# A decoder layer on one core: ScalarE as a second emptier of PSUM banks, the first tile's lines kept on chip, one bias folded into another, and a newly drawn order

## The chip, the cores and the metric

The kernel runs on one core of a Trainium2 chip. The metric is the device time of one execution, in microseconds (us), as the median of several runs. A core has TensorE (PE, matrix products, writes PSUM), VectorE (DVE), ScalarE (ACT), GpSimd (POOL) and SyncE (SP, which here only issues DMAs). Each engine works through its own queue in order; engines wait for each other by semaphores.

## The reference

One decoder layer over x (2048 tokens, 256 features) with a context of 1601 tokens, in float32. The middle step of the first part is what the change touches most.

```python
x = x + self_attn(layernorm(x)); x = x + cross_attn(layernorm(x), ctx); x = x + moe(layernorm(x))

# self attention, 16 heads: queries and keys are six-number "lines"
q1 = bg @ W1_q.T; q2 = bg @ W2_q.T            # bg = [x, previous row of x]; 4 numbers per head
k1 = x @ W1_k.T;  k2 = x @ W2_k.T
q = lines(q1, q2); k = lines(k1, k2)          # p1[i]*p2[j] - p1[j]*p2[i] over 6 pairs, divided by its norm
attn = softmax(causal(einsum(q, J6 k)) * 6**-0.5)
v = x @ Wv.T + bv
out = (attn @ v) @ Wo.T + bo
# cross attention: 16 heads of 16 features, softmax(q k^T) v over 1601 keys, output projection + bias
# moe: 16 experts of 64 tokens, chosen from 6 rounds of Sinkhorn normalisation, gelu, scatter-add
```

## The kernel before

The 2048 tokens are four tiles of 512 tokens, each of four blocks of 128. The work of all engines comes from one list, PLAN, which build_plan() draws up before the kernel is built: it holds ten streams of steps (x, lines, ctx, keys, ones, max, query, weights, scores, pv) with assumed costs, and again and again takes the step whose weighted cost is lowest. Every engine then walks the same PLAN and issues its part of each step. The weights W set the order; nothing is reordered at run time.

The steps that matter here:

- **prep of a tile**: load four blocks of x (`x_load`, SP), mean and variance (`stats`, DVE, and a power on POOL), `norm` (DVE, L1177), `x_turn` (PE transposes into a PSUM bank, L1651; DVE copies it to `xn_t`, L1187), `project` (PE, L1660 and L1663: the line components and the values of a block; DVE adds the value bias bv into `v_self`, L1198, and copies the components to `raw`, L1201). `carry` and `carry_out` hand the last column of one tile to the next.
- **lines of a tile**: three parts on DVE. Part 0 is 24 products of 128x64 (L1218, L1220) for a tile. Part 1 subtracts, sums the squares and takes 1/sqrt by an integer start and three Newton steps of four instructions (L1119 to L1125). Part 2 scales and splits each number into three bf16 parts (L1234 to L1238) in `line_parts`, which lies in even_region. `line_turn` (PE, L1670, a block each) transposes the parts, DVE copies them (L1246), SP stores them to `line_d` in DRAM (L841), and `line_load` brings them back in another arrangement, 24 small DMAs a tile (L741), to `q_line` and `k_line` in self_region: 36 rows, six slots of six components. The products of the slots add up to a product of nearly float32 accuracy. For tile 0 SP and ACT issue 12 of the loads each.
- **ctx_k, ctx_v**: keys and values of the context (PE, L1636, L1645). DVE splits the keys into three parts (`split`: L1139, L1140, L1142, L1143), SP stores them (L802). `x_query` is the same for the queries of the cross attention.
- **scores, pv**: a quad is a group of four heads on one block of keys. PE makes the scores of two heads (L1588 self, L1584 cross) in one of two PSUM buffers, ACT takes the exponential to `probs` (L1050), POOL masks the diagonal block in the self attention (L979), PE multiplies with the values into the bank `po` (L1608). ACT empties `po` after each group of four heads (L1062).
- **join**: `o_turn`, `a_turn`, `out_proj` turn the attention's output, divide it by its sum and project it; DVE empties all three. bo is added to xb by POOL (`bias`, L955) before that.
- **max**: the score maxima of the cross attention, 1024 banks, each four small matmuls (L1702) and a reduction on DVE (L1294).
- After the last pv come the router and the experts, in fixed order.

Ten kinds of step share three PSUM banks g0 to g2 in rotation (G_USE counts them; `g_full` says that PE has filled one, `g_free` that DVE has emptied one). All are emptied by DVE, in PLAN's order. So a bank that DVE empties late holds PE up three uses later. The first self scores wait for all 24 loads of tile 0.

## Time and profile before

| | us |
|---|---|
| median of 3 runs | 1194.92 |
| the runs | 1191.08 to 1196.68 |
| the profiled execution's own time | 1202.16 |
| its span | 1200.4 |
| PE busy | 1110.4 (93%) |
| DVE busy | 874.8 (73%) |
| ACT busy | 708.1 (59%) |
| POOL busy | 153.7 (13%) |
| first self scores on PE | 90.62 |
| mean granted TensorE clock (share of full) | 0.965 |

The profile describes one execution, which lies 7.24 us above the median of the runs. Its busy times count an engine as busy from an instruction's start to its end; PE's overlap in a pipeline. "PEclk" is the clock that TensorE was granted, 1.00 being 2.4 GHz. A name such as cross_region or even_region covers several tensors that share the memory: ctx_sb, parts_ctx and line_t lie in cross_region, raw, lines and line_parts in even_region. The idle time behind an instruction in square brackets is that of its engine just before it, with what ended it.

### The profile page before, as it was taken

How to read it: one execution, taken by the hardware profiler on the slowest of the kernel's cores; microseconds unless marked ns; L12 is line 12 of the kernel's file. 1: busy time of each engine (PE TensorE's matmuls, PEld its weight loads, DVE VectorE, ACT ScalarE, POOL GpSimd, SP SyncE). 2: the span in 40 equal slices, each digit the busy share in tenths (PEclk: the TensorE clock that was granted, in tenths of full speed). 3: DMA queues.
4: the chain of work that ended last, by engine and by line, in shares of the span. 5: the costliest groups of instructions: out<-in, count | busy, mean ns of one | idle time of the engine just before them, and what ended most of it. 6: DMA issues, size and time to landing. Idle time of an engine off the chain costs nothing.

```text
span 1200.4 us, 30294 instructions
## 1 busy us (share of the span) xinstructions
PE 1110.4 (93%) x12556; PEld 519.3 (43%) x12556; DVE 874.8 (73%) x2062; ACT 708.1 (59%) x792; POOL 153.7 (13%) x260
## 2 busy tenths in 40 slices
PE   4677998999999999999999999999999999788797
PEld 2342442332333333444555455555454442566354
DVE  5888458378878888898888888788888980477431
ACT  0005648787767877667866787677775789110011
POOL 3005243212101111000001000010001000101322
PEclk8886899999999999999999999999999999998899
DMA  4141268511111000104122201111111000195794
GB/s 169 31 129 46 80 110 120 134 45 46 33 35 57 16 15 1 51 21 138 30 94 70 91 13 30 51 47 30 30 29 54 16 16 2 42 365 119 214 353 106
DMA packets 85080, 92.32 MB, mean 77 GB/s; under 512 B 20448, under 2 KB 77472, under 8 KB 84944
## 3 DMA queue, kind: packets, MB, share of 16 engines
q1 hardware_dynamic: 78568, 81.35, 24.2%
q10 hardware_dynamic: 4584, 6.88, 1.8%
q0 software_dynamic: 1792, 2.16, 1.0%
q8 instruction: 99, 1.62, 0.6%
q14 instruction: 37, 0.30, 0.1%
HBM read 74.73 MB, written 15.63 MB: 75 GB/s over the span
## 4 chain that ended last, share of the span: by engine, by line
PE 80%; DVE 11%; issue 3%; ACT 3%; POOL 1%; another core or an unknown queue 1%; DMA 0%; SPq 0%; DVEq 0%; ACTq 0%
PE po L1608 24%; PE g L1702 16%; PE scores L1584 14%; PE scores L1588 6%; PE g L1687 3%; ACT probs L1050 3%; PE g L1817 2%; PE g L1793 2%; PE g L1660 2%; PE g L1651 2%; PE g L1677 1%; PE g L1693 1%; PE scores L1617 1%; POOL probs L979 1%; PE g L1670 1%
## 5 line engine op out<-in xcount | busy, mean ns | idle before, releaser
L1050 ACT ACTIVATE probs<-scores 128x1024 f32<-128x1024 f32 (+2 forms) x736 | 676.7, 967 | 297.4 <-PE scores L1588 160.8
L1294 DVE TENSOR_REDUCE mx<-g 128x1 f32<-128x400 f32 (+1 forms) x1024 | 527.2, 568 | 73.3 <-PE g L1702 63.2
L1702 PE MATMUL g<-cross_region,even_region 96*32 96x400 bf16 (+1 forms) x4096 | 306.2, 336 | 0.2
L1584 PE MATMUL scores<-even_region,cross_region 99*32 99x512 bf16 (+1 forms) x3264 | 251.9, 379 | 4.4 <-ACT probs L1050 4.4
L1608 PE MATMUL po<-probs,cross_region 128*32 128x512 f32 (+1 forms) x1664 | 223.2, 593 | 0.8 <-ACT probs L1050 0.8
L1702 PEld LDWEIGHTS g<-cross_region,even_region 96*32 96x32 bf16 x4096 | 118.7, 95 | 179.5 <-DVE mx L1294 74.1
L1608 PE MATMUL po<-probs,self_region 128*32 128x512 f32 (+3 forms) x1280 | 155.1, 559 | 8.7 <-POOL probs L979 8.0
L1584 PEld LDWEIGHTS scores<-even_region,cross_region 99*32 99x32 bf16 (+1 forms) x3264 | 96.0, 96 | 104.5 <-issue 47.3
L1588 PE MATMUL scores<-self_region 36*128 36x512 bf16 (+3 forms) x640 | 107.0, 361 | 7.7 <-ACT probs L1050 7.1
L947 POOL TENSOR_TENSOR rstd<-mv,half 128x1 f32<-128x1 f32 x48 | 27.2, 566 | 586.7 <-DVE mv L1135 586.4
L979 POOL TENSOR_SCALAR_AFFINE_SELECT probs<-probs 128x256 f32<-128x256 f32 x128 | 61.9, 491 | 263.4 <-ACT probs L1050 262.7
L1588 PEld LDWEIGHTS scores<-self_region 36*128 36x128 bf16 x640 | 27.7, 94 | 130.1 <-ACT probs L1050 89.5
L1608 PEld LDWEIGHTS po<-probs,cross_region 128*32 128x32 f32 (+1 forms) x1664 | 55.8, 110 | 25.6 <-ACT probs L1050 4.0
L1085 ACT ACTIVATE even_region<-scores 128x1024 f32<-128x1024 f32 x4 | 4.1, 1024 | 94.6 <-remote 71.0
L1617 PE MATMUL scores<-xbo_sb,ident 128*128 128x256 f32 x190 | 51.1, 422 | 0.0
L1608 PEld LDWEIGHTS po<-probs,self_region 128*32 128x32 f32 x1280 | 30.8, 111 | 39.7 <-POOL probs L979 17.1
L1651 PE MATMUL g<-ident,xn 128*128 128x128 f32 x96 | 21.7, 310 | 27.5 <-DVE xn L1177 25.4
L1268 DVE RECIPROCAL rsum<-g 128x16 f32<-128x16 f32 x32 | 8.1, 255 | 48.2 <-PE g L1677 48.0
L1617 PEld LDWEIGHTS scores<-xbo_sb,ident 128*128 128x128 f32 x190 | 39.2, 213 | 6.2 <-issue 0.2
L1279 DVE TENSOR_TENSOR xb<-g,xb 128x256 f32<-128x256 f32 x32 | 13.6, 425 | 32.1 <-PE g L1687 31.3
L1660 PE MATMUL g<-wself_sb,xn_t 128*128 128x512 f32 x64 | 33.5, 649 | 2.4 <-DVE rest L1140 2.4
L1187 DVE COPY xn_t<-g 128x256 f32<-128x256 f32 x48 | 20.2, 421 | 17.2 <-PE g L1651 17.0
(270 smaller groups left out, 878.4 us busy)
## 6 DMA issues: line engine op xcount, KB each, us to landing
cross_region<-in_w SPq DMA_DIRECT2D x16, 1024.0 KB, 12.1
even_region<-xq_d SPq DMA_DIRECT2D x192, 64.0 KB, 2.3
self_region<-in_w ACTq DMA_DIRECT2D x6, 1024.0 KB, 8.7
self_region<-in_w SPq DMA_DIRECT2D x6, 1024.0 KB, 13.3
cross_region<-xk_d SPq DMA_DIRECT2D x24, 200.1 KB, 10.2
xb<-in_x SPq DMA_DIRECT2D x32, 128.0 KB, 3.0
xb<-x_d SPq DMA_DIRECT2D x32, 128.0 KB, 2.4
probs<-in_w SPq DMA_DIRECT2D x4, 1024.0 KB, 13.0
```

Of the source, the lines that this page charges most:

```text
L947: pool.tensor_tensor(rstd[:, u % 4:u % 4 + 1], mv[:, u % 4, 1:2], half[:, 0:1], ALU.pow).then_inc(rstd_ready, 1)
L979: pool.affine_select(out=d, in_=d, compare_op=ALU.is_ge, fill=0.0, base=0, pattern=[[0, 2], [1, P]], channel_multiplier=-1).then_inc(mask_ ...
L1050: act.activation(probs[0:rows, s % 4, :, off:], ps[s % 2][0:rows, :, off:], ACT.Exp, scale=LSCALE if QUADS[n][0] == "self" else 1.0).then_ ...
L1294: dve.reduce_max(mx[:, k % 2, b, h, c:c + 1], g[:, 0:n_keys], AX_X).then_inc(g_free, 1)
L1584: mm = pe.matmul(ps[s % 2][c:c + n_keys, a, :], k_cross[0:NS * DH + 3, h, i * P + c:i * P + c + n_keys], rhs, start=True, stop=True)
L1588: mm = pe.matmul(ps[s % 2][0:rows, a, off:], lhs, rhs, start=True, stop=True)
L1608: mm = pe.matmul(po[32 * a:32 * a + 32, off:], v[0:rows, i, h * VW:h * VW + 32], probs[0:rows, s % 4, a % 2, off:], start=(i == 0), stop=e ...
L1617: pe.matmul(ps[0][:, 0, 0:D], ident[:, :], xbo_sb[:, :], start=True, stop=True)
L1651: mm = pe.transpose(g[:, k * P:(k + 1) * P], xn[:, norm_no[u] % 2, k * P:(k + 1) * P], ident[:, :])
L1660: pe.matmul(g[:, :], xn_t[:, k, c + 1:c + 1 + P], wself_sb[:, k, 0:512], start=(k == 0), stop=False)
L1687: mm = pe.matmul(g[:, 0:D], attn_t[:, k, :], (wo_sb if step[1] == "self" else wxo_sb)[:, k, :], start=(k == 0), stop=(k == DK - 1))
L1702: mm = pe.matmul(g[q:q + 32, 0:n_keys], q_max[k % 2][0:NS * DH, h, b * P + q:b * P + q + 32], k_cross[0:NS * DH, 4 * (k % 4) + h, start:st ...
```

## The change

1. **ACT as a second emptier.** For nine kinds of step (ctx_k, x_query, ctx_v, x_turn, project, line_turn, a_turn, gate, slot_turn) the planner chooses DVE or ACT (`BY[step]`). A second semaphore `g_free_act` counts ACT's, and `wait_freed` waits for the right one. A split that ACT shares is cast by ACT, subtracted by DVE, cast again by ACT, subtracted by DVE.
2. **Tile 0's lines stay on chip.** In place of line_turn, store and load, ACT copies the query parts and DVE the key parts, 12 copies of 128x192 each, into the slot arrangement in `probs` (`copy_to_slots`); PE transposes that directly, 8 steps of 8 transposes (`slot_turn`), each emptied by one copy of 100x1024 to `q_line` or `k_line`. The unused columns are zeroed once at the start.
3. **bv into bo.** Since the weights of a softmax row add up to one, bv @ Wo is added once to bo (`bias_row`: two matmuls and an addition). The values are then only copied.
4. **Lines.** Part 0 takes 16 products in place of 24 (three pairs that share component 0 go in one instruction). A Newton step is three instructions (two scalar_tensor_tensor) in place of four. `raw` may be overwritten once part 0 has read it (`raw_read`).
5. **Small moves.** bv and log_temp are loaded from ACT's queue as columns. `carry_out` comes earlier; the last one is dropped.
6. **Order.** The weights W are others, and the costs and conditions in the planner follow the points above.

```diff
@@ planner
-W = dict(start=0.252, hungry=2.38, fed=0.0138, act_near=0.2601, max=2.2344, max_ahead=0.05, max_from=72.59,
+W = dict(hungry=0.714, fed=0.0083, act_near=0.2211, max=3.7538, max_ahead=0.0147, max_from=72.59, max_end=8.352,
...
-    x_steps = prep(0) + prep(1) + prep(2) + join("self", 0) + prep(3) + query(0)
+    x_steps = prep(0) + prep(1) + [("bias_row",)] + prep(2) + join("self", 0) + prep(3) + query(0)
...
+        if j == 0:
+            line_steps += [("slots", j)] + [("slot_turn", b, side) for b in range(BPT) for side in range(2)]
+            continue
...
+                if step[0] in EITHER:
+                    got = place(step, free, "ACT")
+                    choices.append((name, step, got, "ACT", W["act_late"] if ("scores", 0) in at else W["act_early"]))
@@ waiting for a bank
+        def wait_freed(eng, *steps):
+            for sm in (g_free, g_free_act):
+                counts = [FREED[st][1] for st in steps if FREED[st][0] is sm]
+                if counts:
+                    eng.wait_ge(sm, max(counts))
@@ slots
+        def copy_to_slots(copy, side):
+
+            for s, part in enumerate((Q_SLOTS, K_SLOTS)[side]):
+                src = line_parts.rearrange("p (b s) q (a e c) -> p b s q a e c", s=2, e=2, c=NC)
+                dst = slotted.rearrange("p s (b a) c -> p s b a c", b=BPT)
+                for e in range(2):
+                    c = 64 * e + s * NC
+                    last = copy(dst[:, side, :, :, c:c + NC], src[:, :, side, part, :, e, :])
+            return last
@@ ScalarE
-            act.wait_ge(s_w["rest"], 112)
+            def empty(step):
...
+                elif kind == "project":
+                    b = step[1]
+                    act.wait_ge(v_ones, 4)
+                    if b >= BPT:
+                        act.wait_ge(raw_read, b // BPT)
+                    act.copy(v_self[:, b, 0:H * VW].rearrange("p (h v) -> p h v", h=H)[:, :, 0:DH],
+                             g[:, 256:512].rearrange("p (h d) -> p h d", h=H))
+                    act.copy(raw[:, b % BPT, :], g[:, 0:256]).then_inc(g_free_act, 1)
...
+                elif step == ("slots", 0):
+                    act.wait_ge(lines_split, 1)
+                    last = copy_to_slots(act.copy, 0)
+                    last.then_inc(slots_q, 1)
...
-                elif step == ("line_load", 0, 1):
-
-                    for r in range(4):
-                        act.wait_ge(line_stored[r], 16)
-                    load_line_side(act, 0, 1)
@@ VectorE
                 for _ in range(3):
                     link(dve.tensor_tensor(t, y, y, ALU.mult))
-                    link(dve.tensor_tensor(t, t, v, ALU.mult))
-                    link(dve.tensor_scalar(t, t, -0.5, 1.5, ALU.mult, ALU.add))
-                    link(dve.tensor_tensor(y, y, t, ALU.mult))
+                    link(dve.scalar_tensor_tensor(out=t, in0=t, scalar=-0.5, in1=v, op0=ALU.mult, op1=ALU.mult))
+                    link(dve.scalar_tensor_tensor(out=y, in0=t, scalar=1.5, in1=y, op0=ALU.add, op1=ALU.mult))
...
+            dve.memset(slotted.rearrange("p s n c -> p (s n) c")[:, :, NS * NC:64], 0.0).then_inc(v_ones, 1)
+            dve.wait_ge(s_w["bv"], 16 * DK)
+            dve.tensor_copy(attn_t[:, :, :], bv_col.unsqueeze(2).broadcast_to((P, DK, P))).then_inc(bias_col, 1)
...
+                            dve.tensor_tensor(lv[:, :, side, :, near], one[:, :, :, 0:1].broadcast_to((P, BPT, H, 3)),
+                                              two[:, :, :, 1:4], ALU.mult)
@@ TensorE
                 if kind == "self" and g == 0 and i == 0 and e == 0:
-                    pe.wait_ge(lines_loaded[j], 16 * 24)
+                    if j:
+                        pe.wait_ge(lines_loaded[j], 16 * 24)
+                    else:
+                        wait_freed(pe, *[("slot_turn", b, side) for b in range(BPT) for side in range(2)])
...
+                    for a in range(H // 2):
+                        mm = pe.transpose(gb[0:100, a * P:(a + 1) * P], slotted[:, side, b * H // 2 + a, :], identb[:, :])
```

TensorE's queue up to the first self scores, before. x_turn is `g<-ident,xn`, project `wself_sb,xn_t`, ctx_k and ctx_v `g<-cross_region`; this is the part behind tile 1's projections:

```order
L1651 MATMUL g<-ident,xn 128x128 x4
L1636 MATMUL g<-cross_region 128x512 x2
L1645 MATMUL g<-cross_region 128x256 x8
L1670 MATMUL g<-identb,even_region 96x128 x24
L1636 MATMUL g<-cross_region 128x512 x4
L1645 MATMUL g<-cross_region 128x256 x8
L1636 MATMUL g<-cross_region 128x512 x2
L1660 MATMUL g<-wself_sb,xn_t 128x512 x2
L1663 MATMUL g<-wself_sb,xn_t 128x128 x2
L1651 MATMUL g<-ident,xn 128x128 x2
```

and the same part now, down to the first scores and what is placed among them:

```order
L1848 MATMUL g<-wo_sb,attn_t 128x256 x2
L1806 MATMUL g<-cross_region 128x512 x4
L1815 MATMUL g<-cross_region 128x256 x4
L1821 MATMUL g<-ident,xn 128x128 x2
L1843 MATMUL g<-identb,probs 100x128 x24
L1821 MATMUL g<-ident,xn 128x128 x2
L1843 MATMUL g<-identb,probs 100x128 x40
L1815 MATMUL g<-cross_region 128x256 x4
L1758 MATMUL scores<-self_region 128x512 x4
L1831 MATMUL g<-wself_sb,xn_t 128x512 x2
L1834 MATMUL g<-wself_sb,xn_t 128x128 x2
L1821 MATMUL g<-ident,xn 128x128 x2
```

Before, all four projections of tile 2 and the last ctx_k stand ahead of the first scores (the shown part ends in the first of them). Now the four projections stand among tile 0's scores, and one bias_row and 64 slot transposes stand where 24 line transposes stood.

VectorE's queue behind part 0 of tile 0's lines, before (the 24 products of tile 0's lines come as L1218, L1220 in turn; the last of them is shown first, and part 1 begins 25 rows behind the last one shown):

```order
L1220 TENSOR_TENSOR even_region<-even_region 128x4x16
L1139 CAST cross_region<-g 128x512
L1140 TENSOR_TENSOR rest<-g,cross_region 128x512
L1142 CAST cross_region<-rest 128x512
L1143 TENSOR_TENSOR cross_region<-rest,cross_region 128x512
L1198 TENSOR_TENSOR self_region<-g,bv_sb 128x16x16
L1201 COPY even_region<-g 128x256
L1187 COPY xn_t<-g 128x2x128
L1177 TENSOR_SCALAR xn<-xb,mv,rstd 128x256
L1198 TENSOR_TENSOR self_region<-g,bv_sb 128x16x16
L1201 COPY even_region<-g 128x256
```

and now, from the last of the 16 products to the beginning of part 1:

```order
L1377 TENSOR_TENSOR even_region<-even_region 128x4x16
L1327 TENSOR_SCALAR xn<-xb,mv,rstd 128x256
L1282 TENSOR_TENSOR rest<-g,cross_region 128x512
L1288 TENSOR_TENSOR cross_region<-rest,cross_region 128x512
L1327 TENSOR_SCALAR xn<-xb,mv,rstd 128x256 x2
L1381 TENSOR_TENSOR even_region<-even_region 128x768
L1382 TENSOR_TENSOR even_region<-even_region 128x768
L1383 TENSOR_REDUCE even_region<-even_region 128x128
```

Tile 1's four projections and its x_turns are no longer in VectorE's queue, and of the first two splits it has only the subtractions; tile 2's stats, which stood ahead of part 1, now come behind part 2.

ScalarE had nothing in its queue ahead of the first exponential but an exp of one column and the 12 loads. Now it has first the casts of two splits, three x_turns, two ctx_v and three projections, and then this:

```order
L1132 COPY self_region<-g 128x16x16
L1134 COPY even_region<-g 128x256
L818 COPY probs<-even_region 128x32x6 x12
L1137 COPY self_region<-g 100x8x128 x3
L1150 COPY cross_region<-g 128x2x16x16
L1194 ACTIVATE probs<-scores 128x1024 x2
L1132 COPY self_region<-g 128x16x16
L1134 COPY even_region<-g 128x256
L1125 COPY xn_t<-g 128x2x128
L1194 ACTIVATE probs<-scores 128x2x384 x2
L1132 COPY self_region<-g 128x16x16
L1134 COPY even_region<-g 128x256
```

So copies out of PSUM now stand between the exponentials of tile 0. Over the whole run ACT takes 8 of 16 projections, 10 of 48 x_turns, 5 of 7 ctx_v, 3 of 8 slot_turns and the casts of 2 of the 16 splits; the last of them are two ctx_v and four x_turns during the self attention of tile 1. From then on its queue is the exponentials and the emptying of po, as before.

## Rows read from the trace of the kernel before

**Rows 1.** Busy time by stretch (us; PEclk granted clock, last GB/s):

```profile
0.00:90.60 90.60, 57.45 (x196) 33.36 (x196) 64.06 (x190) 1.49 (x2) 12.05 (x24) 0.87 0.35 109
90.60:134.50 43.90, 33.67 (x251) 11.81 (x250) 35.55 (x84) 22.80 (x36) 22.97 (x36) 0.69 0.17 45
134.50:200.00 65.50, 60.72 (x412) 24.29 (x410) 39.00 (x108) 42.57 (x54) 21.39 (x33) 0.97 0.67 114
200.00:1000.00 800.00, 791.17 (x10634) 349.05 (x10636) 647.97 (x1419) 603.11 (x655) 65.46 (x128) 1.00 0.16 46
```

**Rows 2.** Timeline, ahead of the first scores, PE (start, us, engine, line, what):

```profile
82.13 3.57 PE L1660 MATMUL g<-wself_sb,xn_t 128*128 128x512 f32 x4 [0.88 <-DVE rest L1140]
...
88.36 1.88 PE L1660 MATMUL g<-wself_sb,xn_t 128*128 128x512 f32 x4
...
90.62 0.60 PE L1588 MATMUL scores<-self_region 36*128 36x512 bf16 x4
```

**Rows 3.** Timeline, DVE, tile 0's lines and around:

```profile
5.26 0.43 DVE L1133 BATCH_NORM_STATS2 bn<-xb 128x6 f32<-128x256 f32 x1 [3.05 <-DMA xb<-in_x]
...
22.68 0.43 DVE L1133 BATCH_NORM_STATS2 bn<-xb 128x6 f32<-128x256 f32 x1
...
25.89 0.41 DVE L1177 TENSOR_SCALAR xn<-xb,mv,rstd 128x256 f32<-128x256 f32 x1
...
29.40 0.27 DVE L1218 TENSOR_TENSOR even_region<-even_region 128x64 f32<-128x64 f32 x1
...
33.61 0.27 DVE L1220 TENSOR_TENSOR even_region<-even_region 128x64 f32<-128x64 f32 x1
...
50.45 0.95 DVE L1224 TENSOR_TENSOR even_region<-even_region 128x768 f32<-128x768 f32 x1
...
57.33 0.23 DVE L1124 TENSOR_SCALAR even_region<-even_region 128x128 f32<-128x128 f32 x1
57.59 0.29 DVE L1125 TENSOR_TENSOR even_region<-even_region 128x128 f32<-128x128 f32 x1
57.91 0.96 DVE L1234 TENSOR_TENSOR even_region<-even_region 128x768 f32<-128x768 f32 x1
...
61.09 0.96 DVE L1238 TENSOR_TENSOR even_region<-even_region 128x768 bf16<-128x768 f32 x1
```

**Rows 4.** Groups on DVE up to 90.6 us:

```profile
L1139 DVE CAST cross_region<-g 128x512 bf16<-128x512 f32 x5 | 3.4, 688 | 1.9 <-PE g L1636 1.7
...
L1246 DVE COPY cross_region<-g 96x768 bf16<-96x768 bf16 x4 | 2.1, 549 | 0.2
```

**Rows 5.** Groups on ACT, whole run:

```profile
L1050 ACT ACTIVATE probs<-scores 128x1024 f32<-128x1024 f32 x608 | 592.1, 1023 | 254.6 <-PE scores L1584 127.3 <-PE scores L1588 126.0
...
L1062 ACT COPY o_region<-po 128x512 f32<-128x512 f32 x32 | 18.8, 588 | 12.2 <-PE po L1608 12.2
...
L1090 ACT COPY self_region<-po 128x256 f32<-128x256 f32 x2 | 0.7, 366 | 0.0
...
L1040 ACT ACTIVATE temp<-temp 128x1 f32<-128x1 f32 x1 | 0.2, 203 | 21.8 <-DMA temp<-in_log_temp 21.8
```

**Rows 6.** Timeline, transposes and an output projection, PE:

```profile
65.22 2.15 PE L1670 MATMUL g<-identb,even_region 128*96 128x128 bf16 x18 [0.91 <-DVE cross_region L1261]
...
135.07 1.13 PE L1687 MATMUL g<-wo_sb,attn_t 128*128 128x256 f32 x4
```

**Rows 7.** Timeline, stores and loads of the lines, SP and ACT queues:

```profile
66.25 2.10 SPq L841 DMA_DIRECT2D line_d<-cross_region  x4
...
70.35 4.81 ACTq L741 DMA_DIRECT2D self_region<-line_d  x12
...
112.38 8.99 SPq L741 DMA_DIRECT2D self_region<-line_d  x24
```

**Rows 8.** Chain of waits, then timeline: masks of tile 0 on POOL.

```profile
111.80 4.18 POOL probs L979 x2
...
116.03 0.65 PE L1608 MATMUL po<-probs,self_region 128*32 128x128 f32 x8 [2.93 <-POOL probs L979]
```

More of the change, by code:

```diff
@@ L353, in place @@
             shape = "rows" if quads[step[1]][0] == "self" else "columns"
-        for engine, us, before, event, lag in work(step):
+        for engine, us, before, event, lag in work(step, by):
             ready = 0.0
@@ L419, in build_plan @@
         if step[0] in G_STEPS:
-            ends = [e for en, us, before, e, lag in work(step) if en == "DVE"]
-            at["bank", used[0]] = new[ends[0]]
+            parts = work(step, by)
+            pe = [n for n, part in enumerate(parts) if part[0] == "PE"][0]
+            at["bank", used[0]] = new["split", split_no[step]] if step in split_no else new[parts[pe + 1][3]]
             used[0] += 1
+            evac[step] = by
         if step[0] == "norm":
```

350 lines of the change are left out of this document (245 added, 105 removed).

## The prediction, made before the changed kernel was run

> **What bounds the kernel now.** I read the busy time by stretch first [rows 1]. From 200 to 1000 us PE is busy for 791.17 of 800 us: PE bounds that stretch, no edit takes work from PE there, and what moves other engines' work in it is worth at most 9 us, more likely nothing. The change must pay, if it does, ahead of 200 us. There PE has three stretches: up to 90.6 us it is busy for 57.45 (33.2 idle, of which 8.9 lie before its first instruction), from 90.6 to 134.5 for 33.67 of 43.9 (10.2 idle), and to 200 for 60.72 of 65.5 (4.8 idle). The first ends with the first self scores at 90.62 [rows 2], the second with tile 1's first scores. In the first, DVE is the busier engine, 64.06 us, and ACT has nothing to do (1.49 us). PE waits there for normed blocks and for banks that DVE hasn't emptied. The granted clock is 0.87 in the first stretch and 0.69 in the second, against 1.00 later [rows 1]; a projection's four long passes take 3.57 us at the lower of the two levels, 1.2 GHz, and 1.88 at 2.4 GHz [rows 2].
>
> So the time is PE's fixed work plus its holes, and the holes depend on when tile 0's lines are ready. Before, they end in DVE's part 2 at 62.05, and then go through stores at 66.25 and 24 loads, the ACT half of which was issued from 70.35 to 75.16 [rows 3, 7]. PE was then given tile 2's projections first, and reached the scores at 90.62.
>
> **First scores, by VectorE's new queue.** DVE ends tile 0's projections as before at 22.68 [rows 3]. At its start it has one more memset, hidden in its 3.05 us of waiting for x [rows 3], and a copy that waits for two small loads; I add 0.5 us (0 to 1.5). Then in order:
> - stats of tile 1, carry, one norm: 22.68 to 26.3, so 3.6 us [rows 3];
> - two splits of which ACT does the casts: 2 x 0.72 us of subtractions on DVE each, by the nearest row a cast (0.69) [rows 4], and one wait each for ACT's second cast, 0.59 for 128x512 [rows 5] plus the way there and back, 0.8: together 4.5;
> - part 0 with 16 products: the 24 before ran from 29.40 to 33.88, 0.18 each [rows 3]. Twelve cost 2.2. For a product of 128x192 there is no row: below 0.18 (128x64), above 0.98 (128x768, the step of 50.45 with its gap). In proportion to length it is 0.33, so 1.3 for four, 3.5 in all (2.9 to 6.1);
> - three norms, 1.3;
> - part 1: 50.45 to 57.91 is 7.5 [rows 3]. Three tensor_scalar instructions of 0.23 and a gap of 0.03 fall away, 0.8. The scalar_tensor_tensor instructions have no row; I take that of a tensor_tensor, 0.29, as floor, and 0.52, the sum of the two that one replaces, as ceiling. 6.7 (to 8.1);
> - part 2 and carry_out: 57.91 to 62.05 and 0.2, so 4.3. This ends at 47.1; before it was 62.05. ScalarE's part and the new place of tile 2's stats give most of these 15 us, the shorter lines 1.6.
> - bias_row, stats of tile 2, carry, norm: 0.5, 3.0, 0.6, to 51.2;
> - 12 copies of 128x192 bf16 into the slots: between 0.18 (128x64) [rows 3] and 0.55 (96x768) [rows 4], 0.3 taken, 3.6 (2.2 to 6.6), to 54.8. ACT's 12 run beside these: between 0.20 (one column) and 0.37 (128x256) each [rows 5], at most 4.4, from 47.1 to 51.5, so hidden;
> - two whole splits at 2.5 (0.69 + 0.69 + 0.43 + 0.69 each, the cast and its neighbours) [rows 4], a ctx_v 0.7, two x_turns and norms 1.9: to 62.4;
> - five of the eight slot_turns: 0.55 x 1024/768 = 0.73 each with a small gap, 4.2 (ACT's three are 1.0 each by the exponential of the same length [rows 5] and lie beside the splits): to 66.6.
>
> First scores at 67 instead of 90.6: 23.6 us earlier. With all low ends it is 62, with the high ones and some waits for PE 76. No store, load or landing of tile 0 is left to be late. PE is the next candidate: it had 57.45 us of work there; four projections (2.16 each at full level, 88.36 to 90.52) [rows 2], two x_turns (0.8) and one ctx_k (1.9) go, 11.3 in all, and bias_row (1.1 like an output projection) and 40 more transposes at 2.15/18 = 0.12 [rows 6], 4.8, come. 52 of 67 us, with its first instruction at 8.9: 6 us of slack, so DVE still ends last, narrowly.
>
> **From there to tile 1.** The 11.3 us that PE put off come among tile 0's scores, where it has 10.2 us of holes (it waits for exponentials and masks). Neither nothing nor everything will fit: added to the stretch are between 0 and 11.3 us; I take 5.8, the middle. So tile 1's scores start at 67 + 43.9 + 5.8 = 116.7, 17.8 us earlier than 134.5. Are tile 1's loads there? Lines of tile 1 start at 67 on DVE, need 3.5 + 0.4 + 6.7 + 4.3 and what the masks take from them, up to 85; they are turned by 90; their 24 loads take 9.0 us to issue [rows 7], now all from SP, landed by about 105. That hides with 12 to spare. Behind SP's loads stand one store of key parts and tile 2's line stores, neither of which is waited for before.
>
> ACT's copies among the exponentials (four projections at 2 x 0.37 or more, two x_turns, all between the first exponentials and mostly beside PE's own projection) I cost at nothing: ACT has 22.80 busy of 43.9 there [rows 1]. If the cover fails this is the third rival. Later ACT takes six more copies, 3 us. In the stretch to 200 and behind, PE's work and its neighbours are the same, so 0 (within 2). The bias fold on DVE exchanges an addition for a copy of the same length, 0. Behind the last pv nothing is moved.
>
> Sum: -23.6 + 5.8 = -17.8. The profiled execution took 1202.16, so it would be 1184.4; that run is 7.24 above the median, so the median comes to 1177.
>
> **Rivals.**
> 1. *The holes are filled, and the clock comes up.* All 11.3 us fit: -23.6. And PE, with fewer pauses, is granted full clock in some of tile 0's stretch: PE's 33.67 busy us stood at 0.69 [rows 1], of which up to 10 could be given back; say 4. Time 1195 - 28 = 1167. For: the holes are as long as the work. Against: the scores wait for exponential and mask in turn, and a projection of 2.2 us is longer than most holes.
> 2. *ScalarE's queue.* A projection's copies stand before exponentials; the copy waits for PE's whole projection (2.2 to 3.9 us), and for tile 2 also for `raw_read`, while scores lie finished. Four times 2.5 us is 10: gain 8, 1187. For: the queue is in order, and three such copies stand between the first eight exponentials. Against: PE does nothing else in that time either.
> 3. *Masks held.* While DVE ran its short products back to back, two masks took POOL 4.18 us, and PE waited 2.93 for them [rows 8]. Now two such runs (tile 1's and tile 2's part 0) lie in tile 0's attention in place of one: 3 to 4 us more, 1181; with tile 1's pass also among the critical masks at most 1185.
>    The Trainium skill, SBUF — State Buffer, "Who interferes with whom", says that a VectorE instruction with two SBUF inputs and a GpSimd instruction that reads SBUF exclude each other for a whole instruction. By that rule the new run of 16 products blocks one more mask pair. The trace agrees in the case of the 4.18 us.
> 4. *The scores don't start early*: a bank is emptied late by one engine and stops both, or the slot copies cost their ceiling; first scores at 82 or later, gain at most 3, 1192.
> 5. *Slower: the clock stays down.* The new stretch of tile 0 holds 33.67 x 0.69 + 8.6 = 32 us of PE work at full level. If PE is kept at 1.2 GHz from its slot transposes, which wait for copies one by one, through tile 0 and 10 us of work of tile 1, that work takes 42 us more than at full level, 14 of which were paid before: 28 lost against 17.8 won, 1205. It decides from 18 us of loss on. For: 0.69, the mean over the same kind of work, says that more than half of the time was at the lower level. Against: the rest was not, and the projections now among the scores are dense work.
>
> **How the numbers follow.** Forecast 0.44, rivals 1 to 5: 0.17, 0.15, 0.09, 0.08, 0.04; 0.03 for what I haven't seen. The range: 1166 holds rival 1 (the high ends of copies don't matter there), 1190 holds rivals 2 and 3 and first scores up to 80. Within 0.5% of 1194.92 is 1189 to 1201, about what a measurement of this kernel can tell from no change. Faster: forecast, 1, 3 and most of 2, 0.84. Same: rival 4 and a rest of 2, 0.11. Slower: 5 and half of the unseen, 0.05.
>
> **What would show it.** First scores at 62 to 76, DVE's part 2 ending near 47, tile 1's scores near 117, PE's idle time ahead of the first scores near 15 to 17 us (from 33), 200 to 1000 as busy as before. Idle time on PE behind `exp` with ACT in a projection copy would show rival 2; long masks beside L1371 to L1377 rival 3; a granted clock of 0.5 to 0.6 from 60 to 110, rival 5. The forecast is wrong if first scores come early and tile 1's don't.

## The result, and the profile after

The changed kernel takes 1176.09 us (median of 4 runs, 1175.68 to 1179.23), the kernel before 1193.59 beside it (4 runs, 1191.08 to 1196.68). The ratio is 0.9857 (95% interval 0.9839 to 0.9876), 17.5 us between the medians. The forecast was 1177, in a range from 1166 to 1190.

Busy time by stretch, changed kernel (columns as in [rows 1]). The stretches are: to the first self scores, to tile 1's first scores, to VectorE's last `shift_t` copy (near the end of the attention), to the end.

```profile
0.00:67.40 67.40, 45.23 (x200) 28.76 (x200) 47.49 (x143) 14.73 (x35) 13.43 (x24) 0.92 0.35 111
67.40:113.70 46.30, 39.10 (x281) 14.85 (x282) 36.52 (x83) 25.79 (x46) 24.19 (x36) 0.85 0.20 56
113.70:975.40 861.70, 846.99 (x10932) 378.33 (x10928) 681.45 (x1511) 638.96 (x703) 84.09 (x161) 0.99 0.20 51
975.40:1174.60 199.20, 171.39 (x1192) 100.43 (x1192) 88.64 (x264) 48.69 (x59) 31.82 (x39) 0.96 0.60 181
```

In the trace of before the same four stretches are 90.6, 43.9, 854.2 and 211.7 us. The last pair is misleading: 12.5 us of the 25.9 between the two profiled executions lie in the tail, whose code the change doesn't touch (the engines run the same number of instructions in it, 1192 on PE and 264 on VectorE). That is why the kernel before was traced again (its experiment is below). In that second trace, taken on the same chip as a second one of the changed kernel, the same stretches are

```profile
0.00:92.20 92.20, 57.92 (x196) 33.47 (x196) 64.08 (x190) 1.49 (x2) 12.01 (x24) 0.85 0.34 107
92.20:137.30 45.10, 33.46 (x252) 11.23 (x250) 35.31 (x84) 22.83 (x36) 23.85 (x36) 0.70 0.17 44
137.30:993.70 856.40, 844.93 (x10921) 371.62 (x10919) 686.25 (x1525) 634.77 (x696) 86.27 (x161) 0.99 0.20 52
993.70:1194.50 200.80, 174.61 (x1192) 102.91 (x1192) 88.20 (x264) 48.76 (x59) 31.85 (x39) 0.95 0.59 180
```

and in the second one of the changed kernel

```profile
0.00:68.40 68.40, 45.90 (x200) 29.48 (x200) 47.70 (x143) 14.63 (x35) 12.08 (x24) 0.93 0.34 109
68.40:113.40 45.00, 40.84 (x281) 15.45 (x280) 36.08 (x83) 25.89 (x46) 23.84 (x36) 0.77 0.20 55
113.40:974.80 861.40, 848.35 (x10936) 378.29 (x10928) 680.89 (x1510) 638.71 (x703) 84.19 (x161) 0.99 0.20 52
974.80:1175.60 200.80, 174.29 (x1193) 102.10 (x1192) 88.84 (x264) 48.78 (x59) 32.27 (x39) 0.95 0.59 180
```

This pair adds up cleanly: -23.8 ahead of the first scores, -0.1 in tile 0's stretch, +5.0 behind it, 0.0 in the tail, -18.9 in all. In the first pair the same differences are -23.2, +2.4, +7.5 and -12.5. So up to the end of the attention the changed kernel is ahead by 13.3 us in one pair and by 18.9 in the other, and the 17.5 between the medians lie between these. Tile 0's stretch holds 29 matmul records more (281 for 252) in the same 45 us, and PE is busy in it for 40.84 us in place of 33.46: the work that was put off went into the holes. Part of the +5.0 is no loss but work that moved past tile 1's first scores: the join of tile 0 begins behind them now. Its first eight transposes `g<-ident,o_region` and two `g<-ident,attn` took PE 2.1 us in tile 0's stretch of the kernel before. In all PE is busy for 3.4 us more behind tile 1's first scores; the rest is holes (13.1 for 11.5).

The head in the changed kernel, VectorE (timeline):

```profile
7.90 0.29 DVE L1306 COPY attn_t<-bv_sb 128x256 f32<-128x256 f32 x1 [4.77 <-DMA bv_sb<-in_bv]
8.11 0.42 DVE L1271 BATCH_NORM_STATS2 bn<-xb 128x6 f32<-128x256 f32 x1
...
25.46 0.43 DVE L1271 BATCH_NORM_STATS2 bn<-xb 128x6 f32<-128x256 f32 x1
...
36.41 0.69 DVE L1288 TENSOR_TENSOR cross_region<-rest,cross_region 128x512 bf16<-128x512 f32 x1 [0.68 <-ACT cross_region L1179]
...
37.67 0.95 DVE L1381 TENSOR_TENSOR even_region<-even_region 128x768 f32<-128x768 f32 x1
...
47.73 0.96 DVE L1398 TENSOR_TENSOR even_region<-even_region 128x768 bf16<-128x768 f32 x1
...
52.47 1.53 DVE L818 COPY probs<-even_region 128x192 bf16<-128x192 bf16 x12
...
64.14 2.48 DVE L1406 COPY self_region<-g 100x1024 bf16<-100x1024 bf16 x4 [0.22 <-PE g L1843]
```

ScalarE's slot copies and PE's first scores:

```profile
48.73 3.13 ACT L818 COPY probs<-even_region 128x192 bf16<-128x192 bf16 x12 [1.77 <-DVE even_region L1398]
67.41 0.61 PE L1758 MATMUL scores<-self_region 36*128 36x512 bf16 x4
```

The first row is new: VectorE stands still for 4.77 us before it has seen x, and its first stats begin at 8.11 in place of 5.26 [rows 3]. Part 2 ends at 48.7 (62.05 before). VectorE's last slot emptying ends at 66.62; PE then still has the end of a ctx_v before it, and the scores begin at 67.41 (90.62 before [rows 2]).

### The profile page after: what moved, and what is told of

It is laid out like the page before. It is cut to its first block, busy times and chain, and to the rows that moved or that the text cites. A ratio compares the mean times of both kernels' runs of the same rounds, so it can differ in the third digit from the quotient of the medians.

```text
span 1174.6 us, 30371 instructions
## 1 busy us (share of the span) xinstructions
PE 1102.7 (94%) x12600; PEld 522.4 (44%) x12600; DVE 854.1 (73%) x1998; ACT 728.2 (62%) x842; POOL 153.5 (13%) x260
## 4 chain that ended last, share of the span: by engine, by line
PE 79%; DVE 13%; issue 3%; ACT 2%; DMA 2%; POOL 1%; SPq 0%; ACTq 0%; DVEq 0%
PE po L1778 24%; PE g L1886 16%; PE scores L1754 14%; PE scores L1758 6%; PE g L1871 3%; PE g L1977 2%; PE g L2001 2%; ACT probs L1194 2%; PE g L1861 2%; PE g L1821 1%; PE g L1865 1%; PE g L1806 1%; DMA xb<-x_d 1%; DVE mx L1465 1%; PE g L1831 1%
## 5 line engine op out<-in xcount | busy, mean ns | idle before, releaser
L1754 PE MATMUL scores<-even_region,cross_region 99*32 99x512 bf16 (+1 forms) x3264 | 254.6, 379 | 3.0 <-ACT probs L1194 3.0
L1886 PEld LDWEIGHTS g<-cross_region,even_region 96*32 96x32 bf16 x4096 | 121.4, 95 | 172.8 <-DVE mx L1465 68.2
L1754 PEld LDWEIGHTS scores<-even_region,cross_region 99*32 99x32 bf16 (+1 forms) x3264 | 100.1, 96 | 95.0 <-issue 41.7
L1787 PE MATMUL scores<-xbo_sb,ident 128*128 128x256 f32 x190 | 47.3, 399 | 0.0
L1778 PEld LDWEIGHTS po<-probs,self_region 128*32 128x32 f32 x1280 | 29.5, 110 | 39.1 <-issue 22.1
L1787 PEld LDWEIGHTS scores<-xbo_sb,ident 128*128 128x128 f32 x190 | 36.6, 199 | 5.0
L1821 PEld LDWEIGHTS g<-ident,xn 128*128 128x128 f32 x96 | 10.5, 145 | 39.7 <-issue 25.3
## 6 DMA issues: line engine op xcount, KB each, us to landing
cross_region<-in_w SPq DMA_DIRECT2D x16, 1024.0 KB, 13.3
self_region<-in_w SPq DMA_DIRECT2D x6, 1024.0 KB, 13.1
```

The costliest lines, as they stand in the source:

```text
L1754: mm = pe.matmul(ps[s % 2][c:c + n_keys, a, :], k_cross[0:NS * DH + 3, h, i * P + c:i * P + c + n_keys], rhs, start=True, stop=True)
L1778: mm = pe.matmul(po[32 * a:32 * a + 32, off:], v[0:rows, i, h * VW:h * VW + 32], probs[0:rows, s % 4, a % 2, off:], start=(i == 0), stop=e ...
L1787: pe.matmul(ps[0][:, 0, 0:D], ident[:, :], xbo_sb[:, :], start=True, stop=True)
L1821: mm = pe.transpose(g[:, k * P:(k + 1) * P], xn[:, norm_no[u] % 2, k * P:(k + 1) * P], ident[:, :])
L1886: mm = pe.matmul(g[q:q + 32, 0:n_keys], q_max[k % 2][0:NS * DH, h, b * P + q:b * P + q + 32], k_cross[0:NS * DH, 4 * (k % 4) + h, start:st ...
```

## The experiments

All but the second start from the changed kernel. "Mark" is VectorE's last `shift_t` copy, 975.4 and 974.9 in the changed kernel's two traces. Each run has one trace. Four of them (long lines, projections first, lines through DRAM in this order, and the last one) ran on a second chip, where the kernel before took 1201.9; their times are compared by their ratio to it. A difference "in us above the changed kernel" is worked out from such ratios, against both of the changed kernel's (0.9857 and 0.9841).

**The changed kernel again** (no edit).

> The changed kernel as it is, timed once more as the yardstick for its neighbours, with a second trace. If the 12.5 us by which the tail behind the last self and cross attention work was shorter in its trace than in that of the kernel before belong to the executions and not to the kernels, its median lies 16 to 19 us under the kernel before's and the tail of this trace (from the first final o_turn to the end) is anything from 160 to 175 us. If the tail is really shorter, it is 162 to 164 again.

Measured 1175.95 us, 16.9 under the kernel before, ratio 0.9841 (0.9815 to 0.9866). From the first final `o_turn` to the end it takes 164.3 us (162.8 in its first trace), which fits both theories; by the mark used here the tail is 200.8 (199.2). The next run decides.

**The kernel before again** (no edit).

> The kernel before, traced once more. Its first trace was 8.6 us above its median, and from its last shift_t copy to the end of the span it took 211.7 us, where four traces of the changed kernel and its near relations took 199.3 to 200.8. Theory: the router and expert part is the same in both kernels and the long tail was that execution's; here it is 199 to 204 us. Rival: the tail is really longer before (211 again), and then 11 of the 17.5 us come from it.

The tail took 200.8 us and the single time is 1196.27. So the tail gives nothing of the gain. Over all traces the tail is 199.2 to 200.9 in nine and 208.6 to 211.7 in five. Four of the five are those of the second chip, the fifth is the first trace of the kernel before, whose chip isn't on record. The same kernel has both tails, so it goes with the chip or the session, not with the kernel.

**The copy of bv later.** VectorE does it behind `carry` of tile 1.

```diff
-            dve.wait_ge(s_w["bv"], 16 * DK)
-            dve.tensor_copy(attn_t[:, :, :], bv_col.unsqueeze(2).broadcast_to((P, DK, P))).then_inc(bias_col, 1)
...
                         dve.tensor_copy(xn_t[:, :, 0], carry[:, :]).then_inc(carried, 1)
+                        if step[1] == 1:
+                            dve.wait_ge(s_w["bv"], 16 * DK)
+                            dve.tensor_copy(attn_t[:, :, :], bv_col.unsqueeze(2).broadcast_to((P, DK, P))
+                                            ).then_inc(bias_col, 1)
```

> Theory: VectorE's queue ends the stretch ahead of the first scores, so its 4.77 us of waiting for bv at the start, of which 2.8 us arrived at the end of tile 0's projections, is lost one for one. With the copy placed behind carry of tile 1 the first stats start near 5.3 (from 8.11), the first scores near 64.7 (from 67.41), and the time falls by 2.8 us, to about 1173.3. Rival: PE has no slack left there, or what is won comes back as a longer wait later (for x, for masks, for the clock): first scores earlier by under 1 us or the time the same within 1 us.

Measured 1176.36 us, ratio 0.9843 (0.9816 to 0.9869): no gain. VectorE, timeline:

```profile
6.96 0.43 DVE L1271 BATCH_NORM_STATS2 bn<-xb 128x6 f32<-128x256 f32 x1 [3.83 <-DMA xb<-in_x]
```

Behind the wait for bv lay a wait for x, 1.7 us longer than in the kernel before (5.26), although x's own load is issued at the same 1.31 us. The stats were early by 1.15 us, and still tile 0's projections ended at 25.41, as without the edit, and the first scores came at 67.79. PE's first projection, in the changed kernel and here:

```profile
13.75 3.24 PE L1831 MATMUL g<-wself_sb,xn_t 128*128 128x512 f32 x4
```

```profile
12.62 3.62 PE L1833 MATMUL g<-wself_sb,xn_t 128*128 128x512 f32 x4
```

PE began 1.13 us earlier, but in this execution its granted clock rose from 1.2 to 2.4 GHz later: the four passes took 3.62 us for 3.24, and the four short ones behind them 1.06 for 0.61. The changed kernel's second trace shows the same: stats at 7.34, 3.62 and 1.06, projections ended at 25.98. So a start that is a microsecond earlier need not arrive at the end of the projections. The theory was half right: the wait was there, but not its whole cause.

**The small loads later as well.** ScalarE issues log_temp and the two columns of bv when x has landed.

```diff
+            act.wait_ge(x_loaded[3], 16)
             act.dma_start(temp[:, 0:1], log_temp.partition_broadcast(P)).then_inc(s_w["temp"], 16)
```

> With the copy of bv moved away (the run before), x itself was waited for until 6.96 us, 1.7 us longer than in the kernel before. Here the three small loads that the change put at the head of ScalarE's queue (log_temp to 128 partitions, bv as two columns, all in pieces of 4 bytes) are issued only once x's first four blocks have landed; the copy of bv stays behind carry of tile 1. Theory: these loads of 4-byte pieces stand in front of x's packets in the DMA engines; the first stats start at 5.2 to 5.5, tile 0's projections end near 22.9 (from 25.4), the first scores are at 64.7 to 65.3 (from 67.4 to 68.4 in five traces) and the time falls by 2 to 3 us, to 1173 to 1174. Rival: x lands late for another reason (the memory banks, the longer queue of the program's start): the stats stay near 7 and the time at 1175 to 1177.

VectorE, then PE, timeline:

```profile
5.34 0.43 DVE L1272 BATCH_NORM_STATS2 bn<-xb 128x6 f32<-128x256 f32 x1 [2.21 <-DMA xb<-in_x]
```

```profile
65.00 0.61 PE L1761 MATMUL scores<-self_region 36*128 36x512 bf16 x4
```

The head is as forecast: stats at 5.34, first scores at 65.00. Three loads in 4-byte pieces, 128 each, had kept x away for 1.6 us. The mark stands at 969.3, 5.5 to 6 us earlier, of which 2.4 to 3.4 come from the head and most of the rest from tile 0's stretch (43.2 us, granted clock 0.96). But the median is 1174.37 (1171.34 to 1176.02), ratio 0.9847 (0.9825 to 0.9869): 1.6 us under the changed kernel on the same chip, within the spread of both. The profiled execution was the fastest of the five; what the others did in place of it no trace shows.

**The keys' load later.** `keys_load` 0 is issued behind the x loads of the cross queries.

```diff
+    move([("keys_load", 0)], ("keys_load", 1))
```

> In the changed kernel the first keys' load (6 transfers of 200 KB) is issued at 154.03, ahead of the four loads of x that the cross queries wait for (156.84); these take 9.2 us to land. Here the keys' load is issued behind them. Theory: this late landing is what holds the queries' norms, then tile 3's lines, and then PE (2.46 us at 192.58, some 3 us in smaller waits from 169 to 175, and a clock of 0.66 to 0.83 after it): the x loads land in 3 us, PE's waits between 165 and 200 fall by at least 3 us and the time by 3 to 6 us. Rival: DVE, busy with tile 3's lines and the projections' copies, gets to the norms no earlier, or PE finds another wait: the time is the same within 1 us.

Measured 1174.33 us, ratio 0.9837 (0.9813 to 0.986). In the changed kernel (x loads on SP at 156.84, stats of the queries, and PE's waits from 165 to 200 us):

```profile
156.84 1.79 SPq L847 DMA_DIRECT2D xb<-x_d  x4
```

```profile
168.11 0.43 DVE L1271 BATCH_NORM_STATS2 bn<-xb 128x6 f32<-128x256 f32 x1
```

```profile
PE scores L1758 <- ACT probs L1194: 3.3, 7, 0.9
PE g L1854 <- DVE even_region L1398: 2.5, 1, 2.5
PE g L1821 <- DVE xn L1327: 1.6, 2, 0.9
```

and in this run (163 to 198 us, all is 2 us earlier from tile 0 on):

```profile
149.58 1.84 SPq L854 DMA_DIRECT2D xb<-x_d  x4
```

```profile
166.11 0.43 DVE L1278 BATCH_NORM_STATS2 bn<-xb 128x6 f32<-128x256 f32 x1
```

```profile
PE scores L1765 <- ACT probs L1201: 3.3, 7, 0.9
PE g L1861 <- DVE even_region L1405: 2.5, 1, 2.5
PE g L1828 <- DVE xn L1334: 1.6, 2, 0.9
```

The loads start 7.3 us earlier, 5.3 of them by the edit, and not one wait is different: the rival holds. VectorE comes to the stats right behind tile 3's 16 products in both. The median is 1.6 us lower, but the ratios (0.9837 and 0.9841) can't be told apart. The chain of waits had put 9.21 us on "DMA xb<-x_d", of which VectorE had waited for nothing.

**Tile 2's products left out.**

```diff
                         for side in range(2):
+                            if j == 2:
+                                last = dve.tensor_copy(lines[:, side, 0, 0:1], raw[:, side, 0:1])
+                                continue
```

> Tile 2's part 0, 16 products, is left out (one element is copied in their place; part 1 then works on other numbers). Theory of the held masks: in the changed kernel these products ran from 86.86 to 90.2 and four masks took POOL 6.01 us (0.41 each when alone), for which PE waited 3.48 us at 91.62. Without them that wait falls to under 1.5 us (the two instructions of 128x768 behind them move forward and can still hold a mask), and the time falls by 2 to 3.5 us. Rival: the masks are held by whatever VectorE does there, or the wait comes back behind ScalarE or in the lower clock: PE's holes in tile 0's stretch are the same in sum, and the time within 1 us.

Masks on POOL, then PE, in the changed kernel:

```profile
86.99 6.01 POOL L1055 TENSOR_SCALAR_AFFINE_SELECT probs<-probs 128x256 f32<-128x256 f32 x4 [0.29 <-ACT probs L1194]
```

```profile
91.62 1.51 PE L1778 MATMUL po<-probs,self_region 128*32 128x384 f32 x8 [3.48 <-POOL probs L1055]
```

and the masks without the products:

```profile
88.31 0.78 POOL L1055 TENSOR_SCALAR_AFFINE_SELECT probs<-probs 128x256 f32<-128x256 f32 x1 [0.30 <-ACT probs L1194]
89.35 2.06 POOL L1055 TENSOR_SCALAR_AFFINE_SELECT probs<-probs 128x256 f32<-128x256 f32 x4 [0.27 <-ACT probs L1194]
```

The wait of 3.48 is gone (longest 1.0 left), and tile 0's stretch takes 41.2 us for 43.2 to 46.3 in six traces with the products in this order. The granted clock differs too, 0.92 here and 0.77 to 0.96 in the six; against the two at 0.96 the stretch is 2.0 us shorter. The time is 1174.47 (ratio 0.9843, 0.9814 to 0.9872), 1.5 us less than the changed kernel, too little to be told by times alone. So the products do hold the masks, and that costs at least about 2 us in the traces.

**VectorE empties every bank, order kept.**

```diff
+    evac.update(dict.fromkeys(evac, "DVE"))
```

> The changed kernel with the same order of steps, but every bank that ScalarE emptied (8 projections, 10 x_turns, 5 ctx_v, 3 slot_turns, the casts of 2 splits) is emptied by VectorE. Theory: VectorE's queue ends the head, so what ScalarE did there comes on top of it: casts 2 x (0.69 + 0.43), three x_turns at 0.42, three ctx_v at 0.65, four projections at 0.84, three slot_turns at 0.7, together 10.9 us, less the 1.4 us for which it waited for ScalarE's casts: first scores near 77 (from 67.4), and 5 to 9 us on the time: 1181 to 1185. Rival: the order and the lines on chip give the gain, and VectorE's holes take this work: first scores under 71, time under 1178.

Measured 1199.99 us, ratio 1.0062 (1.0039 to 1.0084): slower than the kernel before. Stretches, then PE:

```profile
0.00:77.50 77.50, 47.24 (x200) 29.76 (x200) 56.63 (x160) 4.62 (x14) 13.41 (x24) 0.91 0.31 96
77.50:129.10 51.60, 40.52 (x283) 15.52 (x284) 40.30 (x97) 22.50 (x35) 23.14 (x36) 0.77 0.18 49
129.10:997.40 868.30, 849.95 (x10932) 378.06 (x10928) 683.80 (x1517) 636.65 (x697) 84.28 (x161) 0.99 0.20 51
```

```profile
100.11 0.84 PE L1861 MATMUL g<-identb,even_region 128*96 128x128 bf16 x6 [7.02 <-DVE even_region L1405]
```

The head is as forecast to half a us (77.5), but the time is 15 us above the forecast, since the head is less than half of the cost. Tile 0's stretch grows by 5.3 to 6.6 (PE waits 7.02 us for tile 1's part 2), the stretch behind by 6.6 to 6.9. This order works only with ScalarE's help. What an order drawn for VectorE alone would reach isn't shown.

**Long lines.** 24 products and four-instruction Newton steps, as before.

```diff
-                    link(dve.scalar_tensor_tensor(out=t, in0=t, scalar=-0.5, in1=v, op0=ALU.mult, op1=ALU.mult))
-                    link(dve.scalar_tensor_tensor(out=y, in0=t, scalar=1.5, in1=y, op0=ALU.add, op1=ALU.mult))
+                    link(dve.tensor_tensor(t, t, v, ALU.mult))
+                    link(dve.tensor_scalar(t, t, -0.5, 1.5, ALU.mult, ALU.add))
+                    link(dve.tensor_tensor(y, y, t, ALU.mult))
...
+                            for c in range(3):
+                                dve.tensor_tensor(lv[:, :, side, :, near.start + c], one[:, :, :, 0],
+                                                  two[:, :, :, 1 + c], ALU.mult)
...
```

> The changed kernel with the long lines of the kernel before: 24 products of 128x64 in part 0, four instructions in each Newton step. Part 0 ran in 3.4 us with 16 products and 4.5 with 24, part 1 in 6.7 against 7.5. Theory: VectorE's queue ends the head, so both come out one for one: first scores 1.9 us later (69.3 to 70.3), and the time 1 to 2.5 us longer, 1177 to 1178.5. Rival: there is slack in PE's or ScalarE's part of the head, or the spread of tile 0's stretch hides it: within 0.7 us of the changed kernel (1175.3 to 1176.8).

Measured 1193.86 on the second chip, ratio 0.9934 (0.991 to 0.9958), which is 9 to 11 us above the changed kernel's: missed by far. Stretches, then PE:

```profile
0.00:69.10 69.10, 46.33 (x200) 29.24 (x200) 49.55 (x156) 14.64 (x35) 12.07 (x24) 0.90 0.33 108
69.10:119.90 50.80, 42.70 (x281) 15.75 (x280) 39.96 (x104) 25.99 (x46) 26.52 (x36) 0.76 0.18 50
119.90:984.20 864.30, 847.80 (x10932) 379.98 (x10928) 684.07 (x1522) 638.75 (x703) 85.12 (x161) 0.99 0.20 51
```

```profile
86.96 0.53 PE L1856 MATMUL g<-identb,even_region 128*96 128x128 bf16 x6 [1.69 <-DVE even_region L1400]
...
96.77 0.85 PE L1780 MATMUL po<-probs,self_region 128*32 128x384 f32 x8 [2.49 <-POOL probs L1055]
```

The mark is 9 us later, of which 0.7 to 1.7 lie in the head, 4.5 to 5.8 in tile 0's stretch and 3 behind it. Tiles 1 to 3 make their lines too, beside masks that the products hold and in front of banks that PE waits for. In tile 0's stretch PE is busy for 42.7 us (39.1 and 40.8 in the changed kernel) and idle for 8.1 (7.2 and 4.2); the granted clock is 0.76 (0.85 and 0.77). How much of the growth is waiting and how much the clock, these traces don't separate.

**Projections first.** Tile 2's projections, two x_turns, a norm and carry_out stand ahead of the first scores, as before.

```diff
+    x2 = [s for s in plan if s == ("norm", "prep", 11, 11) or s == ("carry_out", 2)
+          or s[0] == "project" and s[1] // BPT == 2 or s[:2] == ("x_turn", "prep") and s[2] in (10, 11)]
+    move(x2, ("scores", 0, 0))
```

> The changed kernel with tile 2's four projections, its last two x_turns, a norm and carry_out placed ahead of the first self scores, as in the kernel before, instead of among tile 0's scores. Theory: that work (9.5 us on PE at full clock) lengthened tile 0's stretch by only 2.4 us, so ahead of the scores it costs 8.5 to 10.5 us and gives back 2 to 3: first scores at 76 to 78.5, tile 1's first scores at 119.5 to 122 (from 113.5), and the time 1181.5 to 1184. Rival: PE's work costs the same wherever it stands, since the holes among the scores are too short for projections: tile 0's stretch is shorter by 7 us or more, time 1175 to 1178.

Measured ratio 0.9911 (0.9884 to 0.9939), 6 to 8 us above the changed kernel's. Stretches:

```profile
0.00:76.40 76.40, 54.33 (x236) 34.31 (x236) 53.69 (x161) 17.81 (x44) 13.39 (x24) 0.93 0.31 100
76.40:117.70 41.30, 31.46 (x246) 10.16 (x244) 29.77 (x65) 22.89 (x37) 23.78 (x36) 0.71 0.20 57
```

First scores 8.0 to 9.1 us later, tile 0's stretch 3.7 to 5.0 shorter, tile 1's first scores at 117.75 (earlier than the 119.5 to 122 expected), the mark 4 us later (979.2): among the scores half of this work is free.

**Lines through DRAM, redrawn order.** Four line_turns, stores and 24 loads for tile 0; the planner draws the list anew.

```diff
-        if j == 0:
-            line_steps += [("slots", j)] + [("slot_turn", b, side) for b in range(BPT) for side in range(2)]
-            continue
...
+                    pe.wait_ge(lines_loaded[j], 16 * 24)
```

> The changed kernel with tile 0's lines sent through DRAM as before (4 line_turns, stores, 24 loads, all loads from SP), everything else kept; the planner draws the order anew with the same weights. Theory: part 2 still ends near 48.7, the turns and stores take until 56, the 24 loads need 10.6 us to issue and land by 72 to 76; PE has tile 2's projections in front, so the first scores come at 74 to 80 in place of 67.4, but with about 8.6 us of work less among tile 0's scores, of which only 2.4 us had lengthened that stretch. So tile 1's scores come 5 to 10 us later than 113.7, and the time is 1180 to 1186. Rival: the work that is put off fills the gap either way, and the lines on chip are worth under 2 us: time 1175 to 1178.

Measured 1221.01 us, ratio 1.0239 (1.0204 to 1.0273). First scores 73.86 and tile 1's 119.34, about as forecast; but from there to the mark it takes 901.6 us (861.7 and 861.4 in the changed kernel), and the time is missed by 35 us. PE is busy for only 42.37 of 50 us from 150 and 70.38 of 100 from 200. The list that the same weights give for other steps is bad much later. This says nothing of the lines; the next run does.

**Lines through DRAM, this order**, with the projections first.

```diff
+    gone = [s for s in plan if s[0] in ("slots", "slot_turn")]
...
+    plan[plan.index(("slots", 0)):plan.index(("slots", 0))] = [("line_turn", b) for b in range(BPT)]
+    plan[plan.index(("slot_turn", 0, 0)):plan.index(("slot_turn", 0, 0))] = [("line_load", 0, 0), ("line_load", 0, 1)]
+    for s in gone:
+        plan.remove(s)
```

> As the run with the projections first, and tile 0's lines go through DRAM as in the kernel before (four line_turns in the place of the slot copies, the loads, all 24 from SP, in the place of the first slot_turn). The order of all other steps is the changed kernel's, so this is what the run with a redrawn order was to show and could not (there 40 of the 45 us were lost between tile 1 and the end). Theory: the loads are issued by 69 and landed by 73, while PE has the projections until about 76: the path through DRAM is hidden, VectorE is even freed of 12 slot copies and 5 emptyings, and the time equals that of the run with the projections first within 2 us. So the lines on chip are worth what they allow the order to do, not the transfer's own time. Rival: the loads land at 80 or later: first scores at 82 to 86, time 1187 to 1191.

Measured ratio 0.9886 (0.9862 to 0.9911), the mark at 980.1 (979.2 with the projections first). PE:

```profile
75.80 0.60 PE L1766 MATMUL scores<-self_region 36*128 36x512 bf16 x4 [2.19 <-DMA self_region<-line_d]
```

The loads land just behind the projections (PE waits 2.19 us for them). Beside the projections the way through DRAM costs nothing that these runs can tell; so the lines on chip pay, as far as the runs show, by letting the scores start before the projections, at 67.4 to 68.5.

**Both head edits and two line_turns later.**

```diff
+    move([("line_turn", 12), ("line_turn", 13)], ("pv", 45))
```

> The run with the small loads and the copy of bv later, and in addition tile 3's first two line_turns two steps later in the order (behind pv of quad 44), because PE waited there for the end of part 2 in all traces of the changed kernel (2.5 or 1.3 us at 192 us) while scores and a pv that were ready stood behind. Theory: this wait falls to under 0.7 us, and with the head's gain the time is 1171 to 1173.5. Rival: the scores and pv moved ahead only find their own wait for exponentials, and the head's gain is again lost in the spread of tile 0's stretch: 1174 to 1176.

Measured ratio 0.9831 (0.9802 to 0.9859). PE, here and in the run without this edit:

```profile
187.69 0.87 PE L1864 MATMUL g<-identb,even_region 128*96 128x128 bf16 x12
```

```profile
187.08 0.51 PE L1857 MATMUL g<-identb,even_region 128*96 128x128 bf16 x6 [2.45 <-DVE even_region L1401]
```

The wait is gone, as expected, but from tile 1's first scores to the mark it takes 861.7 us (861.1 without this edit), so nothing is left of it at the mark, 969.6. This has the lowest ratio of all versions; that it beats the changed kernel (0.9841 and 0.9857) isn't shown, since the intervals overlap.

## Why the prediction was right, point by point

- *What bounds it, and where it pays.* Right. From tile 1 on PE is as busy as before (98.3% and 98.5% of the stretch, 98.6% and 98.7% before); all of the gain lies ahead.
- *First scores, 67.* Measured 67.41 and 68.45, in part by luck: errors cancel. The start was taken at 0.5 (0 to 1.5) and cost 2.8 (3.3 in the second trace): the step "a copy that waits for two small loads" was mis-sized, since it priced the copy and not the landing, nor what these loads do to x. The twelve slot copies were taken at 3.6 with 2.2 as the low end and took 1.53, 0.13 each: below the bound. A row of 128x64 f32 products was no floor for a bf16 copy. From there to the slot_turns it took 9.2 in place of 7.6, 1.81 of it a wait for PE's x_turn. Most other steps came out as worked out: 16 products 3.4 (3.5), part 1 6.7 (6.7), so the two-operation instruction costs what a tensor_tensor does (0.29), half splits 4.0 (4.5). The low end of the sum was misadded: the low ends named in the list give 64, not 62.
- *PE has 6 us of slack there.* It has more: 45.23 us busy in place of 52, and 22.2 idle where 15 to 17 were forecast. The projections, x_turns and ctx_k that went had taken 17.0 us in the trace of before, since part of them ran at the lower clock level (3.57 for four passes [rows 2]); the sum took 11.3, all at the upper level. And the slot transposes added 3.5 in place of 4.8. VectorE's queue sets the head's end, within the 0.8 us of PE's ctx_v: 10 us more for ScalarE's banks came through in full (77.54), 1.9 us more for long lines as 0.7 to 1.7 (69.10).
- *Put-off work, 5.8 of 11.3.* Mis-sized: 2.4 in the first pair of traces, 0 in the second. This was rival 1's step, and so tile 1's scores came at 113.7 in place of 116.7. The projections' run puts the free part at about half when it is measured back to front.
- *Later 0 (within 2).* Wrong: 5.0 and 7.5 us, of which about 2.1 are tile 0's join, now behind tile 1's first scores. The forecast counted the work that the change names (projections), not the join that the new list also pushes back. This error and that in the put-off work have opposite signs and nearly cancel, so that the sum of -17.8 agrees with 17.5 between the medians is luck in part. What was taken off for the profiled execution, 7.24, was sound: its excess lay in a tail that the change doesn't touch.
- *"The shorter lines 1.6."* Right for the head (0.7 to 1.7 measured, long lines against short), wrong for the kernel: 9 us by the mark. I had priced VectorE's work behind the first scores at nothing because PE bounds there; but PE still waits for VectorE's lines and for masks there (0.6 and 4.8 us in tile 0's stretch, 4.1 for VectorE between 165 and 200).
- *Rival 2* (ScalarE's queue) didn't come: PE's waits for exponentials in tile 0's stretch are 1.3 and 0.7 us in sum. *Rival 3*: the mechanism is there, with one wait of 3.48 us, but the extra cost that it forecast is not. PE waits for masks for 4.8 and 3.0 us in tile 0's stretch, and waited 5.8 and 7.3 in the kernel before. *Rivals 4 and 5* didn't come; the clock in tile 0's stretch was 0.77 to 0.85, above the 0.69 and 0.70 of before, which is the second half of rival 1.
- The parts don't add up. Taken out one by one from an order drawn for all of them, ScalarE is worth 22 us at the mark, the short lines 9, the place of the projections 4, where all together give 13.3 to 18.9. A likely reason is that each saves time in the same queue, VectorE's, and that without one of them the order no longer fits; no run shows that. What the new weights give alone, and the bias fold, wasn't tested.

## What to carry to other kernels

Where one engine's queue feeds the bounding engine, price its work also behind the point where the other engine seems to bound: here a saving of 1.9 us a tile was worth 9 in all, and ScalarE's share of the emptying 22 where the head showed 10. A transfer that the chain of waits names is a cause only if the engine behind it really waited for it. And before two profiles are compared as a whole, cut them at marks and look for a stretch whose code is the same: its difference belongs to the chip or the execution.

## What the runs showed of the hardware that was not expected

- Loads in 4-byte pieces (bv as two columns, log_temp to 128 partitions) issued beside x's load kept x away until 6.96 us; issued behind it, x was there at 5.34.
- A bf16 copy of 128x192 within SBUF took 0.13 us on VectorE and 0.26 on ScalarE.
- A memset on POOL held VectorE's tensor_scalar within SBUF. POOL, then VectorE, changed kernel:

```profile
172.87 1.43 POOL L1047 MEMSET cross_region<- 32x1604 f32 x1
```

```profile
171.17 0.73 DVE L1327 TENSOR_SCALAR xn<-xb,mv,rstd 128x256 f32<-128x256 f32 x2
172.24 2.21 DVE L1327 TENSOR_SCALAR xn<-xb,mv,rstd 128x256 f32<-128x256 f32 x2 [0.33 <-PE g L1821]
```

  Two norms take 0.73 us alone and 2.21 beside the memset; the second of them took 1.66 (0.41 alone), from 172.79 until 0.14 us behind the memset's end. A tensor_scalar of 128x128 beside the next memset took 1.55 for 0.23, while instructions with two inputs beside the third kept their 0.29. The Trainium skill, SBUF — State Buffer, "Who interferes with whom", says that a tensor_scalar within SBUF can run in a mode that takes both ports, and that then the one that comes second is blocked for the whole instruction of the other. The trace agrees that the two exclude each other; it doesn't confirm the order, since the norm's record begins 0.08 us ahead of the memset's.
- Short products of VectorE with both inputs in SBUF, back to back, held a mask of POOL for almost their whole run: one mask took 3.50 us beside 16 products (0.41 alone), and 0.78 where the products were left out.
- The tail of unchanged code took 199.2 to 200.9 us in nine traces (granted clock 0.95 to 0.96 in it) and 208.6 to 210.3 in the four of the second chip (0.93 to 0.94).
